# A three-layer decoder on one NeuronCore: one program block without barriers, and the FFN weights dequantised beside other work

## The chip, the cores and the metric

The kernel runs on one core of one Trainium2 chip. The metric is the device time of one execution in microseconds (us); lower is better. The profile is that of one execution on the same core. Engines in the profile: PE is TensorE (matmuls), PEld its weight loads, DVE is VectorE, ACT is ScalarE, POOL is GpSimd, SP is SyncE, which issues the transfers here.

## The reference

Inputs are `x` of 4 batches x 512 tokens x 512 features, fp32. Each of three layers ends in a residual sum and a LayerNorm.

```python
# 1: lightning attention: 16 heads of 32, chunks of 128 tokens, a decaying state kv carried over a batch's 4 chunks
q, k, v = rotary(x @ Wq), rotary(x @ Wk), x @ Wv
inter = (q * q_decay) @ kv;  intra = ((q @ k.T) * dmask) @ v
kv = r_C * kv + (k * k_decay).T @ v
x = layernorm(x + rms_norm(attn, rms_w) @ Wo)
# 2: one expert a batch: two int8 "smooth quant" linears, weights fside (512x512) and ctx (512x256)
h = smooth_quant_linear(x, fside);  gate, up = split(h)
x = layernorm(x + smooth_quant_linear(silu(gate) * up, ctx))
#    smooth_quant_linear: s = sqrt(colmax|x| / colmax|w|); x/s and w*s are scaled by row, rounded, clipped, multiplied, rescaled
# 3: FFN with fp4 weights: packed nibbles -> table value * fp16 scale of each group of 128 inputs; I = 1408
h = silu(x @ Wg.T) * (x @ Wu.T);  y = h @ Wd.T;  y = y / rms(y)
x = layernorm(x + y)
```

## The kernel before

Tokens lie on partitions in chunks of 128; a batch has four chunks (NC), the whole input sixteen. A product that must keep fp32 precision is three passes over operands split into a rounded part (`_hi`) and a remainder (`_lo`): ACT copies the rounded part out of PSUM, DVE subtracts it from the same PSUM bank to give the remainder. PSUM has eight banks of 128x512 fp32, `ps[0]` to `ps[7]`. Each engine has its own instruction stream, written out by hand, and executes it in order; what must follow what on another engine is a semaphore wait. Three program blocks follow each other, with a barrier of all engines between them:

- `attention_phase` (L574) runs the 16 chunks of layer 1. Beside them it places the steps of layer 2 for batch 0, by the table `EXPERT0_STEPS` (chunk, part 0 to 2). It also decodes the fp4 nibbles to fp8 values, a sixteenth of them in each chunk (`decode`, `scale_values`), into `shared`. The last chunk is n = 15. After it DVE and ACT finish the LayerNorm of batch 3 of layer 1 (x1), in `z`, and SP stores it.
- `weight_phase` (L1187) makes the FFN weights in 35 pieces: POOL (for some pieces ACT) builds diagonal matrices of the group scales, `scale_diag`; PE multiplies four fp8 blocks with four diagonals into a bank (L1257), which transposes and scales them; ACT writes the hi part (L1240) and DVE the lo part (L1248). Bank m % 8 serves piece m.
- `ffn_phase` (L1263) goes through four batches of 11 inner tiles `it`. For each, PE makes `gate` (12 matmuls, bank 4), `up` (12 matmuls, bank 5) and the `down` product of the tile before (12 matmuls, banks 0 to 3); ACT applies silu, DVE multiplies by up, ACT and DVE split the result into h_hi and h_lo. PE has three places a tile for other work, one after each of these groups of 12, so 33 places a batch, numbered `at` = 3*it + 0, 1, 2. There the steps of layer 2 for the next batch are placed, by the table `EXPERT_STEPS` (name: place), and the output steps of the batch before. On ACT and DVE the same places stand between the silu, multiply and split steps. At the end of a batch PE transposes the next batch's input (`transpose_x2`, L1522). Batches 1 and 2 are a hardware loop.

The steps of layer 2 use two PSUM banks, 6 and 7, in turn, in the order of the list `EXPERT_USES`. Each use waits until the one before it on that bank is drained (`start_use`, `drained`), which is done by the engine that reads the bank: DVE for `ratio` and `scale_x`, ACT for the transposed integers, and so on.

Names that come up again: `rows` broadcasts the column factors into both banks for `scale_x` and `scale_w` (DVE); `max_x`, `max_w` are row maxima (DVE); `round_x`, `round_w` are four activations each (ACT); `clip_x`, `clip_w` are POOL's; `xq01` to `wq23` transpose the integers and ACT copies them out; `w_scale`, `v_scale` broadcast a weight's row scales into a bank. The second linear has the same steps with `a` and `v`.

Of the kernel before, what the change touches and what calls it, by code (L numbers as in the profile page):

```python
# [15 lines left out]
F8 = mybir.dt.float8e4  # L16

# [113 lines left out]
LINKS = 14  # L131


QUAD = 4


def weight_pieces():


    pieces = []  # L140
    for t in range(0, GU_TILES, QUAD):
        for g in range(NK):
            pieces.append(("gu", g, t * P, min(QUAD, GU_TILES - t), t * E + g * P, E, g * GU_TILES + t))
    for k in range(NI):
        pieces.append(("dn", k, 0, NK, GU_TILES * E + k * P, I, NK * GU_TILES + k * NK))
    return pieces


PIECES = weight_pieces()


class Expert:

    def __init__(self, nc, sem, memory):
# [15 lines left out]
        self.gated, self.summed = sem("gated"), sem("summed")  # L170
        self.x2_shift, self.x2_done, self.mom = sem("x2_shift"), sem("x2_done"), sem("e_moments")
# [1447 lines left out]
```

## Time and profile before

| | |
|---|---|
| median of 3 runs (lowest to highest) | 849.53 us (847.71 to 850.36) |
| the profiled execution: device time, span | 849.56 us, 847.8 us |
| busy share of the span | PE 87%, PEld 70%, DVE 54%, ACT 43%, POOL 25% |
| mean granted TensorE clock | 0.942 |
| instructions | 11955 |

The span runs from the first to the last instruction. A timeline row gives the start in us, the length in us, engine, line, operation, what it writes and reads, how many instructions were merged (x4), and in square brackets the idle time of that engine just before it and who ended it. In a row of windows the five "busy (count)" pairs are PE, PEld, DVE, ACT and POOL; behind them stand the granted clock of TensorE (1.00 is 2.4 GHz, 0.50 is 1.2 GHz), the share of DMA busy and GB/s. "L12" is a line of the kernel before. Matmuls overlap, so that the length of one (0.39 us for 128x512) is more than the distance between two.

### The profile page before, as it was taken

To read this page: it belongs to the slowest core of one execution; us is meant where nothing else is said; L and a number is where in the kernel's file an instruction comes from. 1 tells how busy PE (TensorE), PEld (TensorE's weight loads), DVE (VectorE), ACT (ScalarE), POOL (GpSimd) and SP (SyncE) were. 2 spreads that over 40 slices of the span, in tenths; PEclk is the share of its full clock that TensorE was granted. 3 is DMA by queue.
4 is the path that set the end of the run, shared out by engine and by line. 5 is a ranking of instruction groups with operands and counts; after the bars stand their busy time and mean duration, and the time that the engine had idled before them with its cause. 6 is when DMAs were issued, how large, how long until landed. Compare 5 with 4: busy or idle time off the path is not lost.

```text
span 847.8 us, 11955 instructions
## 1 busy us (share of the span) xinstructions
PE 738.6 (87%) x4662; PEld 597.1 (70%) x4662; DVE 459.4 (54%) x899; ACT 362.3 (43%) x583; POOL 212.1 (25%) x242
## 2 busy tenths in 40 slices
PE   5899989989997994269999989999979998899993
PEld 4688867778875783137877767877767777688882
DVE  4567567765656757376725346745358444433214
ACT  4353343555444362573532453543463625431312
POOL 1453444445334353390101210110200111200000
PEclk9899999999999998558999989999999999999997
DMA  8400100023011100401020120030120020100201
GB/s 310 174 27 1 39 13 14 2 84 104 2 26 63 50 2 1 148 1 51 1 74 1 50 99 1 1 124 0 49 99 0 24 99 1 50 1 1 100 0 49
DMA packets 25402, 41.08 MB, mean 48 GB/s; under 512 B 5002, under 2 KB 7690, under 8 KB 25226
## 3 DMA queue, kind: packets, MB, share of 16 engines
q1 hardware_dynamic: 23194, 37.40, 13.2%
q10 hardware_dynamic: 2160, 3.02, 1.0%
q8 instruction: 33, 0.54, 0.3%
q14 instruction: 15, 0.12, 0.0%
HBM read 28.88 MB, written 11.53 MB: 48 GB/s over the span
## 4 chain that ended last, share of the span: by engine, by line
PE 42%; DVE 6%; ACT 4%; issue 2%; DVEq 0%; ACTq 0%
PE ps L1498 27%; PE ps L1508 10%; PE ps L477 2%; DVE silu L1431 1%; PE ps L468 1%; DVE act_s L318 1%; PE ps L457 1%; ACT silu L1356 1%; ACT h_hi L1339 1%; ACT xb L248 1%; DVE xc L1444 1%; ACT q2T L224 0%; DVE e_stats L399 0%; PE ps L1522 0%; PE ps L449 0%
## 5 line engine op out<-in xcount | busy, mean ns | idle before, releaser
L1498 PE MATMUL ps<-x2T_lo,wgu_hi 128*128 128x512 f32 x352 | 143.6, 408 | 5.2 <-DVE x2T_lo L1421 5.2
L1498 PE MATMUL ps<-x2T_hi,wgu_lo 128*128 128x512 f32 x352 | 139.1, 395 | 0.0
L1498 PE MATMUL ps<-x2T_hi,wgu_hi 128*128 128x512 f32 x352 | 139.1, 395 | 0.0
L1431 DVE TENSOR_TENSOR silu<-ps,silu 128x512 f32<-128x512 f32 x44 | 30.4, 691 | 136.0 <-PE ps L1498 130.8
L1080 PE MATMUL ps<-wqkv_lo,xT_hi 128*128 128x512 f32 x192 | 81.8, 426 | 9.3 <-DVE wqkv_lo L960 5.7
L1498 PEld LDWEIGHTS ps<-x2T_lo,wgu_hi 128*128 128x128 f32 x352 | 67.7, 192 | 20.9 <-DVE x2T_lo L1421 6.2
L1498 PEld LDWEIGHTS ps<-x2T_hi,wgu_lo 128*128 128x128 f32 x352 | 67.2, 191 | 14.6
L1498 PEld LDWEIGHTS ps<-x2T_hi,wgu_hi 128*128 128x128 f32 x352 | 67.5, 192 | 13.6
L1080 PE MATMUL ps<-wqkv_hi,xT_hi 128*128 128x512 f32 x192 | 76.8, 400 | 0.0
L1080 PE MATMUL ps<-wqkv_hi,xT_lo 128*128 128x512 f32 x192 | 76.7, 399 | 0.0
L1345 ACT ACTIVATE silu<-ps 128x512 f32<-128x512 f32 x44 | 26.2, 595 | 114.7 <-PE ps L1498 114.7
L897 POOL TENSOR_TENSOR rot<-qkv,tab 128x256 f32<-128x256 f32 x64 | 44.6, 730 | 117.9 <-ACT qkv L810 117.9
L1339 ACT ACTIVATE h_hi<-silu 128x512 fp32r<-128x512 f32 x44 | 27.8, 631 | 105.9 <-DVE silu L1431 105.8
L1508 PE MATMUL ps<-wdn_lo,h_hi 128*128 128x512 f32 x176 | 70.0, 398 | 0.0
L1508 PE MATMUL ps<-wdn_hi,h_lo 128*128 128x512 f32 x176 | 68.7, 390 | 0.0
L1508 PE MATMUL ps<-wdn_hi,h_hi 128*128 128x512 f32 x176 | 68.5, 389 | 0.0
L280 POOL TENSOR_SCALAR act_s<-act_s 128x1024 f32<-128x1024 f32 (+1 forms) x16 | 13.3, 830 | 183.6 <-ACT act_s L218 183.4
L1011 DVE TENSOR_TENSOR masked<-ps,mask 128x512 f32<-128x512 f32 x64 | 39.8, 684 | 32.0 <-PE ps L1118 32.0
L1080 PEld LDWEIGHTS ps<-wqkv_lo,xT_hi 128*128 128x128 f32 x192 | 37.3, 194 | 20.0 <-DVE wqkv_lo L960 6.1
L810 ACT ACTIVATE qkv<-ps 128x512 f32<-128x512 f32 x48 | 28.6, 597 | 51.3 <-PE ps L1080 51.3
L1415 DVE TENSOR_TENSOR h_lo<-silu,h_hi 128x512 fp32r<-128x512 f32 x44 | 30.5, 694 | 32.9 <-ACT h_hi L1339 32.9
L1257 PE MATMUL ps<-scale_diag,shared 128*128 128x128 f16 x132 | 19.3, 308 | 27.6 <-POOL scale_diag L1220 27.6
(168 smaller groups left out, 1519.3 us busy)
## 6 DMA issues: line engine op xcount, KB each, us to landing
w<-in_fside_BxS2xS_dram SPq DMA_DIRECT2D x4, 1024.0 KB, 6.4
x_dram<-xb SPq DMA_DIRECT2D x4, 1024.0 KB, 4.5
xc<-x_dram SPq DMA_DIRECT2D x4, 1024.0 KB, 5.9
x_in<-in_x_dram SPq DMA_DIRECT2D x15, 256.0 KB, 3.1
xb<-x_dram SPq DMA_DIRECT2D x3, 1024.0 KB, 5.5
out_dram<-xc SPq DMA_DIRECT2D x3, 1024.0 KB, 4.3
z<-in_x_dram SPq DMA_DIRECT2D x3, 768.0 KB, 5.0
x_dram<-z SPq DMA_DIRECT2D x3, 768.0 KB, 4.0
```

The costliest lines, as they stand in the source:

```text
L477: last = nc.tensor.matmul(self.bank(use)[:, :], q1T[:, k, c * P:(c + 1) * P], q2T[:, k, :], start=(k == 0), stop=(k == kt - 1))
L810: nc.scalar.activation(qkv[:, n % 2, p * E:(p + 1) * E], bank(u, n)[:, :], ACT.Copy)\
L897: nc.gpsimd.tensor_tensor(rot[:, m], v, f, ALU.mult).then_inc(rot_a, 1)
L1011: nc.vector.tensor_tensor(masked[:, j], in_groups(f"s{j}", n), mask[:, j], ALU.mult)\
L1080: last = nc.tensor.matmul(bank(u, n)[:, :], lhs, rhs, start=(k == 0 and m == 0), stop=(k == NK - 1 and m == 2))
L1257: last = nc.tensor.matmul(ps[m % len(ps)][:, t * P:(t + 1) * P], values[:, start + t * stride:start + t * stride + P], scale_diag[:, m % D ...
L1339: nc.scalar.activation(h_hi[:, it % 2, :], silu[:, it % 2, :], ACT.Copy).then_inc(h_hi_done, 1)
L1345: nc.scalar.activation(silu[:, it % 2, :], ps[4][:, :], ACT.Silu).then_inc(silu_done, 1)
L1415: nc.vector.tensor_tensor(h_lo[:, it % 2, :], silu[:, it % 2, :], h_hi[:, it % 2, :].bitcast(F32), ALU.subtract).then_inc(h_lo_done, 1)
L1431: nc.vector.tensor_tensor(silu[:, it % 2, :], ps[5][:, :], silu[:, it % 2, :], ALU.mult)\
L1498: last = nc.tensor.matmul(dst[:, :], lhs, rhs, start=(k == 0 and n == 0), stop=(k == NK - 1 and n == 2))
L1508: last = nc.tensor.matmul(ps[c][:, :], lhs, rhs, start=(it == 0 and n == 0), stop=(it == NI - 1 and n == 2))
```

## The change

The three blocks become one, without a barrier. Each engine runs its attention program and then its FFN program. Four things move:

1. Memory is laid out by hand: `weights`, the hi and lo parts of all FFN weights, lies over the buffers of attention (`wqkv`, `xT`, `mask`, `kv`, `wo`, `z` and others), so a piece may be written only when what lies below it is done. Piece 24 on lies over `z` and waits for the store of x1.
2. The weight phase is gone. Its 35 pieces are placed among other work: 0 to 5 in the last chunk (`PIECES_BESIDE`, banks 2 to 4), 6 to 34 at places 0 to 28 of the first FFN batch (`PIECE_STEPS`), on the banks 6 and 7 of layer 2. POOL makes all diagonals, into four buffers instead of eight: 0 to 3 after chunk 14, 4 to 6 after chunk 15, and then piece m+1's at the place of piece m, behind the clip and gate steps of that place.
3. The last part of x1's LayerNorm for batch 3 runs at place 1 of the first FFN batch on ACT and DVE (`late`); SP's stores of it now stand ahead of its first FFN transfers. The second batch's fside weight is loaded in the last chunk.
4. The steps of layer 2 are retimed: `w_scale` and `v_scale` come before the integers, the second linear's steps up to one place earlier, the sums `xb + act_s` of batches 1 to 3 go from POOL to DVE, `normalise` from place 31 to 30. The hardware loop is written out. In chunk 15 the residual of the chunk stands ahead of the expert's sums on DVE, and the rms root ahead of its normalise on ACT.

```diff
-                "round_w": 10, "clip_w": 10, "xq01": 13, "xq23": 14, "wq01": 15, "wq23": 16, "w_scale": 16,
+                "round_w": 10, "clip_w": 10, "w_scale": 11, "xq01": 13, "xq23": 14, "wq01": 15, "wq23": 16,
...
-                "clip_v": 25, "aq": 27, "vq": 28, "v_scale": 28, "y01": 29, "rescale_y01": 29, "add01": 29, "y23": 30,
-                "rescale_y23": 30, "add23": 30, "sum01": 30, "sum23": 31, "e_root": 31, "shift": 31, "normalise": 31}
+                "clip_v": 25, "v_scale": 25, "aq": 26, "vq": 27, "y01": 28, "rescale_y01": 28, "y23": 29,
+                "rescale_y23": 29, "sum01": 29, "sum23": 29, "e_root": 30, "shift": 30, "normalise": 30}
...
+PIECES_BESIDE = {(15, 0): (0, 1), (15, 1): (2, 3), (15, 2): (4, 5)}
+PIECE_BANKS = (3, 4, 3, 4, 3, 2)
+FIRST_BESIDE = len(PIECE_BANKS)
+PIECE_STEPS = {m - FIRST_BESIDE: m for m in range(FIRST_BESIDE, len(PIECES))}
+LATE_PIECE = 24
+ROWS_OPEN = range(13, 21)
+DIAGS = 4
...
+def expert_bank(use):
+    if use[0] == "piece":
+        return (use[1] + (use[1] in ROWS_OPEN)) % 2
+    return EXPERT_USES.index(use[1]) % 2
...
+    def diagonals(self, pool, m):
+        if m >= DIAGS:
+            _, full, _, at = self.use(m - DIAGS)
+            pool.wait_ge(full, at + 1)
...
+    def product(self, pe, m):
+        kind, where, k, tiles, _ = PIECES[m]
+        bank, full, drained, at = self.use(m)
+        pe.wait_ge(self.diag_done, m + 1)
+        if at > 0:
+            pe.wait_ge(drained, at)
+        for n in range(self.count(m)):
...
+            last = self.nc.tensor.matmul(bank[:, n * P:(n + 1) * P], values, self.diag[:, m % DIAGS, n, :],
+                                         start=True, stop=True)
+        last.then_inc(full, 1)
+    def hi(self, act, m):
+        act.wait_ge(full, at + 1)
+        if m == LATE_PIECE:
+            self.wait_last_x1(act)
+        self.nc.scalar.activation(self.parts(m)[0], bank[:, 0:self.count(m) * P], ACT.Copy).then_inc(self.hi_done, 1)
+    def lo(self, dve, m):
+        dve.wait_ge(self.hi_done, m + 1)
+        self.nc.vector.tensor_tensor(lo, bank[:, 0:self.count(m) * P], hi.bitcast(F32), ALU.subtract)\
+            .then_inc(drained, 1)
...
         def sums(b, chunks):
             for c in chunks:
+                if b > 0:
+                    self.wait_drained(dve, b, f"y{c}")
+                    nc.vector.tensor_tensor(xb[:, c, :], xb[:, c, :], act_s[:, c, :], ALU.add).then_inc(self.summed, 1)
...
+            if n == CHUNKS - 2:
+                for m in range(DIAGS):
+                    weights.diagonals(pool, m)
+        for m in range(DIAGS, FIRST_BESIDE + 1):
+            weights.diagonals(pool, m)
...
+    def place(expert_steps, output_steps, b, piece=None, late=()):
+        def run(at):
...
+            if b == 0 and piece and at in PIECE_STEPS:
+                piece(PIECE_STEPS[at])
+            if b == 0 and at == 1:
+                for step in late:
+                    step()
...
+        for b in range(B):
+            transpose_x2(b)
+            beside = place(steps, {}, b, lambda m: weights.product(pe, m))
+            for it in range(NI):
+                inner_tile(b, it, beside)
+            down(b, NI - 1)
```

Three places show the new order. The rows are instructions of one engine, with the semaphores that each waits for.

POOL at the end of the last chunk, before (`sq` is the squares' sum, `xb` the sum of layer 2):

```order
L927 TENSOR_TENSOR sq<-sq 128x256 [waits ps1_drained]
L929 TENSOR_TENSOR sq<-sq 128x128 [waits sq_halved]
L291 TENSOR_TENSOR xb<-xb,act_s 128x512 [waits bank6_drained]
L291 TENSOR_TENSOR xb<-xb,act_s 128x512 [waits bank7_drained]
L580 UNCONDITIONAL_BRANCH
```

POOL there now:

```order
L1080 TENSOR_TENSOR sq_65<-sq_65 128x256 [waits ps1_drained]
L1082 TENSOR_TENSOR sq_65<-sq_65 128x128 [waits sq_halved]
L340 TENSOR_TENSOR xb<-xb,act_s 128x512 [waits bank6_drained]
L340 TENSOR_TENSOR xb<-xb,act_s 128x512 [waits bank7_drained]
L690 TENSOR_TENSOR scale_diag_95<-ident_ones,scale_cols_78 128x512 [waits ps3_full]
L690 TENSOR_TENSOR scale_diag_95<-ident_ones,scale_cols_78 128x512 [waits ps4_full]
```

The two new rows are the diagonals of pieces 4 and 5. PE's products of these pieces stand ahead of the last chunk's output product `y` (L1324).

PE at place 7 of the first FFN batch, before (`rows`, then `down`):

```order
L457 MATMUL ps6<-ident_ones,small 128x128 [waits columns_ready,bank6_drained]
L457 MATMUL ps6<-ident_ones,small 128x128 x3
L457 MATMUL ps7<-ident_ones,small 128x128 [waits columns_ready,bank7_drained]
L457 MATMUL ps7<-ident_ones,small 128x128 x3
L1508 MATMUL ps0<-wdn_lo,h_hi 128x512 [waits h_lo_done]
```

PE there now:

```order
L505 MATMUL ps6<-ident_ones,small 128x128 [waits columns_ready,bank6_drained]
L505 MATMUL ps6<-ident_ones,small 128x128 x3
L505 MATMUL ps7<-ident_ones,small 128x128 [waits columns_ready,bank7_drained]
L505 MATMUL ps7<-ident_ones,small 128x128 x3
L707 MATMUL ps6<-scale_diag_95,values_gu_76 128x128 [waits bank6_drained,w_diag_done]
L707 MATMUL ps6<-scale_diag_95,values_gu_76 128x128 x3
```

Piece 13's product comes directly behind the rows, on the same bank 6.

SP's first transfers after the last chunk's, before and now:

```order
L1317 DMA xb<-x1_dram 128x4x512 [waits x2T_ps,x2_stored]
L1320 DMA w<-in_ctx_1024_dram 128x4x256 [waits bank7_full]
```

```order
L921 DMA x2_dram<-xb 128x4x512 [waits x2_done]
L878 DMA x1_dram<-z_75 128x512 [waits x1_done]
L878 DMA x1_dram<-z_75 128x3x512 [waits x1_done]
L1395 DMA xb<-x1_dram 128x4x512 [waits x2T_ps,x2_stored]
L1398 DMA w<-in_ctx_1024_dram 128x4x256 [waits bank6_full]
```

The load of the next batch's x1 now stands behind the two stores of batch 3's x1, which wait for the LayerNorm that was moved to place 1.

## Rows read from the trace of the kernel before

**Rows 1.** Windows of core 0: length, engines' busy time (count), PEclk, DMA share, GB/s.
```profile
352.20:383.20 31.00, 19.29 (x132) 11.60 (x133) 21.74 (x35) 23.46 (x53) 28.68 (x30) 0.50 0.21 68
386.50:502.30 115.80, 107.78 (x519) 86.69 (x517) 57.50 (x97) 48.29 (x79) 14.12 (x13) 0.99 0.13 41
502.30:515.20 12.90, 12.90 (x49) 10.46 (x50) 8.04 (x12) 6.63 (x9) 0.00 (x0) 0.85 0.26 83
623.70:634.80 11.10, 11.10 (x49) 9.16 (x50) 8.13 (x12) 6.66 (x9) 0.00 (x0) 1.00 0.29 94
```

**Rows 2.** Timeline of PE after the last chunk: start, length, engine, line.
```profile
353.25 1.61 PE L1257 MATMUL ps<-scale_diag,shared 128*128 128x128 f16 x12 [18.57 <-POOL scale_diag L1220]
383.22 3.65 PE L1522 MATMUL ps<-ident_ones,xb 128*128 128x128 f32 x16 [1.68 <-PEq L1196]
```

**Rows 3.** Timeline of ACT, last chunk.
```profile
331.52 0.60 ACT L854 ACTIVATE sq<-ps 128x512 f32<-128x512 f32 x1 [0.76 <-DVE o_lo L1023]
333.78 2.05 ACT L818 ACTIVATE shared<-magnitude 128x1056 fp8e4<-128x1056 f16 x1 [1.67 <-DVE magnitude L953]
338.84 2.93 ACT L248 ACTIVATE xb<-xb,small 128x512 f32<-128x512 f32 x4 [0.44 <-DVE small L408]
```

**Rows 4.** Timeline of POOL, last chunk.
```profile
332.19 0.99 POOL L927 TENSOR_TENSOR sq<-sq 128x256 f32<-128x256 f32 x1 [4.06 <-ACT sq L854]
334.03 2.50 POOL L291 TENSOR_TENSOR xb<-xb,act_s 128x512 f32<-128x512 f32 x2
```

**Rows 5.** Timeline of DVE, last chunk.
```profile
333.67 1.27 DVE L399 BATCH_NORM_STATS2 e_stats<-xb 128x6 f32<-128x512 f32 x2
341.95 0.16 DVE L970 RECIPROCAL rms<-rms 128x1 f32<-128x1 f32 x1 [3.14 <-ACT rms L862]
```

**Rows 6.** Lines of the weight phase: count, duration ns min/median/max, starts, shapes.
```profile
L1220 POOL TENSOR_TENSOR scale_diag<-ident_ones,shared x30: 620/1048/1052, 352.2 to 379.8; 128x512 f16<-128x512 f32 x27, 128x256 f16<-128x256 f32 x3
L1257 PEld LDWEIGHTS ps<-scale_diag,shared x132: 102/149/152, 353.2 to 381.1; 128*128 128x128 fp8e4 x132
L1240 ACT ACTIVATE wgu_hi<-ps x24: 378/594/598, 353.9 to 371.4; 128x512 fp32r<-128x512 f32 x20, 128x256 fp32r<-128x256 f32 x4
L1248 DVE TENSOR_TENSOR wgu_lo<-ps,wgu_hi x24: 415/687/693, 354.5 to 372.1; 128x512 fp32r<-128x512 f32 x20, 128x256 fp32r<-128x256 f32 x4
```

**Rows 7.** DMA issues of the page: count, KB each, us to landing.
```profile
xb<-x_dram SPq DMA_DIRECT2D x3, 1024.0 KB, 5.5
```

**Rows 8.** Timeline of DVE, batch 0, from its maxima of x1.
```profile
396.39 2.00 DVE L318 TENSOR_REDUCE act_s<-xb 128x256 f32<-128x1024 f32 x1
408.99 2.48 DVE L350 TENSOR_TENSOR act_s<-xb,ps 128x512 f32<-128x512 f32 x4
414.12 2.45 DVE L350 TENSOR_TENSOR w<-w,ps 128x512 f32<-128x512 f32 x4
```

**Rows 9.** Timeline of PE, batch 0: rows, wq23, columns2.
```profile
406.72 1.03 PE L457 MATMUL ps<-ident_ones,small 128*128 128x128 f32 x8
434.82 1.03 PE L468 MATMUL ps<-ident_ones,w 128*128 128x128 f32 x8
457.45 0.38 PE L449 MATMUL ps<-ident_ones,act_s 128*128 128x128 f32 x2
```

**Rows 10.** Timeline of ACT, batch 0.
```profile
414.23 2.94 ACT L218 ACTIVATE act_s<-act_s,biases,small 128x512 f32<-128x512 f32 x4 [0.38 <-DVE small L366]
436.35 1.25 ACT L224 ACTIVATE q2T<-ps,biases 128x512 bf16<-128x512 f32 x2
472.17 2.08 ACT L218 ACTIVATE w<-w,biases,small 128x256 f32<-128x256 f32 x4 [2.31 <-DVE small L366]
```

**Rows 11.** Timeline of DVE, batch 0, second layer.
```profile
459.81 0.75 DVE L323 TENSOR_REDUCE small<-ps 128x2 f32<-128x256 f32 x2
```

**Rows 12.** Waits of the whole run: us in total, times, longest.
```profile
PE ps L457 <- ACT q2T L224: 8.8, 7, 1.4
```

**Rows 13.** Timeline of PE, end of batch 0.
```profile
498.14 2.49 PE L1522 MATMUL ps<-ident_ones,xb 128*128 128x128 f32 x16 [2.59 <-ACT xb L248]
```

More of the change, by code:

```diff
@@ new lines @@
+USES_OF = {"columns": ("x_colmax", "w_colmax"), "rows": ("x_rows", "w_rows"), "w_scale": ("w_scale",),
+           "xq01": ("xq0", "xq1"), "xq23": ("xq2", "xq3"), "wq01": ("wq0", "wq1"), "wq23": ("wq2", "wq3"),
+           "products01": ("gate_up0", "gate_up1"), "products23": ("gate_up2", "gate_up3"),
+           "columns2": ("a_colmax", "v_colmax"), "rows2": ("a_rows", "v_rows"), "v_scale": ("v_scale",),
+           "aq": ("aq0", "aq1"), "vq": ("vq0", "vq1"), "y01": ("y0", "y1"), "y23": ("y2", "y3")}
@@ L538, in attention_order, with pieces @@
 def attention_order():
+    def pieces(n, part):
+        return (("piece", m - len(PIECES)) for m in PIECES_BESIDE.get((n, part), ()))
     yield from (("xT", 0), ("q", 0), ("k", 0), ("xT", 1), ("v", 0), ("q", 1), ("k", 1))
@@ new lines, in attention_programs, with const @@
+    ident_ones, raw, xb, ps = (memory[name] for name in ("ident_ones", "raw", "xb", "ps"))
+    (x_in, z, tab, mask, rms_col, wqkv_hi, wqkv_lo, wo_hi, wo_lo, halves, magnitude, sign, xT_hi, xT_lo, qkv, kd, rot,
+     kT_hi, kT_lo, qT_hi, qT_lo, qdT, masked, kv_old, kv, o_hi, o_lo, sq, rms, stats, mv, ln) = (
+        memory[name] for name in ATTENTION_TILES)
+    eps = expert.biases[:, 0:1]
+    def const(name):
+        return tab[:, TABLE[name][0] - 2 * P:TABLE[name][1] - 2 * P]
+    ident, ones = ident_ones[:, 0, :], ident_ones[:, 1, :]
@@ new lines, in wait_full, with wait_drained, drain_sem, state_ready @@
+    def wait_full(eng, u, n):
+        m, at = ATTENTION_USE[u, n]
+        eng.wait_ge(full[m], at + 1)
+    def wait_drained(eng, u, n):
+        m, at = ATTENTION_USE[u, n]
+        eng.wait_ge(drained[m], at + 1)
+    def drain_sem(u, n):
+        return drained[ATTENTION_USE[u, n][0]]
+    def state_ready(eng, n):
+        b, c = divmod(n, NC)
+        if c == 0:
+            wait_drained(eng, "kv", n)
+        else:
+            eng.wait_ge(kv_done, b * (NC - 2) + c)
+    def beside(steps, n, part):
+        for name, place in EXPERT0_STEPS.items():
+            if place == (n, part) and name in steps:
+                steps[name](0)
@@ new lines, in beside_pieces, with load_half @@
+    def beside_pieces(step, eng, n, part):
+        for m in PIECES_BESIDE.get((n, part), ()):
+            step(eng, m)
+    def load_half(eng, n, weight, half):
+        ks = slice(half * KH, (half + 1) * KH)
+        eng.dma_start(raw[:, n, ks], weight.rearrange("(k p) n -> p k n", p=P)[:, ks]).then_inc(wqkv_in[n][half], 16)
+    gu_words = a["L0_ffn_gate_up_packed"].rearrange("(t p) w -> p t w", p=P).bitcast(U16)
+    dn_words = a["L0_ffn_down_packed"].rearrange("(t p) w -> p t w", p=P).bitcast(U16)
```

1813 lines of the change are left out of this document (901 added, 912 removed).

## The prediction, made before the changed kernel was run

> **What bounds the kernel now.** I read the windows by stage first, then the timelines around the seams, then those of the first FFN batch. In the FFN TensorE is the bound: in the 115.8 us of the first batch it is busy 107.8 us at a granted clock of 0.99, while DVE, ACT and POOL work 57.5, 48.3 and 14.1 us [rows 1]. There, what PE gets in addition costs its full time, and what the others get costs only where PE waits for them. The weight phase is the opposite: 31.0 us at clock 0.50 (1.2 GHz), with POOL busy 28.7 us of it [rows 1]. Ahead of it PE had been idle 18.57 us [rows 2], through the end of layer 1 on ACT and DVE and a barrier. PE's FFN work starts with the transposes at 383.22 [rows 2]. So the seam is worth much. The question is what the 35 pieces cost in the places they get.
>
> **The seam: what goes.** Times are those of the trace before. In the last chunk pieces 0 to 3 come ahead of the attention product: four products and a wait for bank 4, about 1.9 us later than before (my estimate: 4 x 0.3, and 0.7 for the bank). The square on ACT, before at 331.52 [rows 3], then ends at about 334.0. POOL follows with its two squares' sums (332.19 to 334.03, 1.8 us) and the expert's sums, 2.50 us [rows 4], and only then come the diagonals of pieces 4 and 5, 1.05 us each [rows 6]: 340.6. PE stands in front of these pieces with its output product behind them. After the products, ACT's and DVE's parts take until 342.6; the decode on DVE takes 2.3 us (the square starts at 331.52 and the conversion, which waits for the decode, at 333.78) and the conversion 2.05 us [rows 3]: 347.0. Then the rms root (0.3), residual and its statistics (1.7), the expert's four statistics (2 x 1.27 [rows 5]), 1.7 us of small steps, and normalise, 2.93 us [rows 3]: 356.2. Without the order on POOL it would be some 6 us earlier, but DVE's residual, before at 341.95 and behind the expert's sums [rows 5], now also stands ahead of them. Gain: 383.22 - 356.2 = 27.0 us. The transposes after it start at the low clock as before, since PE idles there again.
> The moved `v_scale` and `w_scale` save 0.9 us more in attention: PE waited for ACT ahead of L457 7 times for 8.8 us in all [rows 12], one of them there.
>
> **The products.** A piece is four matmuls of 128 columns. At clock 0.50 one takes 0.149 us of weight load [rows 6]; at full clock I take half, 0.3 us a piece. Bounds: 0.2 us, a quarter of what 512 columns take (11.1 us for 49 of them is 0.227 each [rows 1]), and 0.6 us, the low clock. 27 pieces' worth in the first batch (29, of which four are half) are 8.1 us (5.4 to 16).
>
> **What the first batch waits for.** On ACT a piece costs 0.59 us, on DVE 0.69, on POOL 1.05 [rows 6]: 17, 20 and 30 us more, which the idle time of the three would hold. What it doesn't hold is the order: a product stands in PE's stream with its wait, and PE goes no further until the bank is free and the diagonal built. A group of 12 matmuls is 2.72 us (12 x 0.227). I walk the queues with the durations of the rows, t = 0 at the first gate matmul.
> - Places 1 to 6. Maxima of w (2.0 us, as those of x1 [rows 8]) stand ahead of a piece on DVE, and the late LayerNorm on ACT (2.9 us, as normalise [rows 3]): PE waits 1.5 and 1.6 us at places 3 and 4. The late LayerNorm ends at 14.1; SP stores it and only then issues the load of x1, which takes 5.5 us [rows 7] and lands at 20.0. Before, DVE began the maxima of x1 at 396.39 [rows 8], t = 10. Now it stands at them until 20.1, with piece 9's lo part behind, whose bank the product at place 5 needs: 4.5 us. The second maxima follow: 1.7 us at place 6 and 0.4 for piece 12. Sum 9.7.
> - Places 7 and 8. The rows end at 406.72 + 0.8 [rows 9], and `scale_x`, which drains their bank, ran from 408.99 for 2.48 us, to 411.5 [rows 8]. Piece 13 is on that bank: 4.0 us and some issue. Piece 14 waits for `scale_w`, before at 414.12 for 2.45 us [rows 8], with the row maxima ahead of it. PE's next group is only 2.7 us: another 4.0. Sum 8.1.
> - Places 10 and 11. The diagonals of pieces 16 and 17 stand on POOL behind `clip_x` and `clip_w`, and these behind four activations, 2.94 us [rows 10]: 2.9 and 2.2 us. Sum 5.1.
> - Places 13 to 18. Six pieces behind transposes or products on the same bank. An example is wq23: PE at 434.82 [rows 9], drained by ACT at 436.35 + 1.25 [rows 10], so 2.0 us after the transposes' end. In all 2.0, 0.4, 0.7, 2.1, 0.2, 1.1: sum 6.5.
> - Places 22 to 24. Column maxima's transposes at 457.45 [rows 9], their bank drained at 459.81 + 0.75 [rows 11]: 2.6 us; then `scale_a` 1.6 and `scale_v` 0.8. Sum 5.0.
> - Places 25 to 28. `v_scale` is drained by ACT behind `round_v`, 2.08 us [rows 10], and that behind h_hi: 4.0 us. Then 0.3, 1.3, 2.2. Sum 7.8.
>
> The stalls are 42.2 us. They take the place of three waits that the batch had, 3.8 us by the same timelines. The batch's end: normalise now stands on ACT ahead of the last tile's h_hi, and the shift on DVE ahead of its multiply, behind sums which DVE now adds itself (4 x 0.6). So h_lo comes 12.6 us after the last gate began, where PE is ready after 8.2: a stall of 4.4 us. In return the transposes no longer wait for normalise (2.59 us before [rows 13]) and the splits come earlier: together -0.4 us. First batch: 8.1 + 42.2 - 3.8 - 0.4 = +46.1 us.
>
> **The other batches.** In the second and third, `w_scale` and `v_scale` no longer wait 1.3 us each ([rows 12], 8.8 / 7); at `v_scale` about 1 us comes back, since max_w's twin and round_v stand ahead. With the 0.4 at the end, 2.1 us each: -4.2. The last batch is unchanged.
>
> **The sum** against the profiled execution, 849.56 us (the median of the runs is 849.53): 849.6 - 27.0 - 0.9 + 46.1 - 4.2 = 863.6. I forecast 864 us.
>
> **A rule on the clock.** The same 49 matmuls took 11.1 us at clock 1.00 and 12.9 us at 0.85, where PE had waited for the transposes' splits before [rows 1]: 1.8 us for one fall. The sum has none of that in it.
> The Trainium skill ("TensorE: Matmul & The Clock Gate", "A second HAM failure mode: psum-queue depth-cycling") says that PE's small idle times between groups, while it cycles through PSUM banks, can make its clock swing between the two levels. That is the order this change makes, and the 12.9 us row agrees with the direction. By the rule the sum would be that of the third rival below, by the row of the first batch (0.99 in spite of small waits) that of the forecast.
>
> **Rivals.**
> 1. The pieces hide. If the products find banks and diagonals ready, the first batch pays only 8.1 us and still loses its 3.8 us of waits: 849.6 - 27.9 + 8.1 - 3.8 - 0.4 - 4.2 = 821 us. For it: the idle time of ACT, DVE and POOL. Against it: the pairs of rows above show the drains after PE's arrival. The place that decides is the first batch, and the change is faster than before when its stalls stay under 42.2 - 14.0 = 28 us.
> 2. Half of the stalls. They are chained, and a wait at one place may pay for the next: 21 us gives 842 us.
> 3. The clock falls at each stall of 4 us or several small ones. Ten falls of 1.8 us: 882 us. For it the 0.85 row; against it that DVE, not PE, sets the time in those stretches.
> 4. The barrier wasn't the cost: the seam keeps more than I think, if PE stands longer behind pieces 4 and 5. The 18.57 us of idle ahead of the weight phase [rows 2] would stay, and only 31.0 - 12 = 19 us go: 872 us. It lies within the range of the forecast.
>
> **Numbers.** Forecast with rival 4: 0.60, own range 852 to 876. Rival 3: 0.14. Rival 2: 0.14, of which 0.02 within 0.3%, since it lies near the border. Rival 1: 0.08. The remaining 0.04 is a coincidence of gains and stalls, no change. A measurement of this kernel tells apart about 0.3%, 2.5 us. Faster: 0.12 + 0.08 = 0.20; same: 0.02 + 0.04 = 0.06; slower: 0.74. The range, 842 to 882, leaves out rival 1 and half of each of its neighbours, about 2 in 10.
>
> **What would show it.** The transposes of the first batch start near 355 (right) or well before 350 (the diagonals of 4 and 5 didn't hold PE). PE's waits list products behind DVE's scaling steps (4 us each at places 7 and 8) and behind POOL. The load of x1 is issued 14 us after the batch's start, and the maxima of x1 start at t = 20. The first batch lasts 160 us instead of 115.8, and the next ones about 2 us less than before. The forecast is wrong if the first batch stays under 144 us.

## The result, and the profile after

| | before | changed |
|---|---|---|
| median (lowest to highest), same chip | 849.37 us (847.71 to 850.36) | 875.33 us (873.02 to 875.97) |
| profiled execution: device time, span | 849.56, 847.8 us | 875.86, 873.2 us |
| mean granted clock | 0.942 | 0.942 |
| first gate matmul of batch 0, 1, 2, 3 (us) | 386.5, 502.3, 623.7, 741.4 | 358.7, 532.5, 650.7, 767.9 |

The changed kernel is slower: ratio 1.0303, 95% interval 1.0284 to 1.0321. The sign and the range of the forecast were right; the rise is 26 us where 14.5 were forecast. By the last line of the table the FFN begins 27.8 us earlier (forecast 27.9), the first batch takes 173.8 us instead of 115.8 (+58.1; forecast +46.1), the next two 3.8 us less together (forecast 4.2), and the last one 1.1 less (forecast 0). So one stage holds the error. The mean granted clock is the same by coincidence: the 31 us at 0.50 of the weight phase are gone, and the first batch has fallen from 0.99 to 0.90.

The batches as windows of the changed kernel (length; busy time and count of PE, PEld, DVE, ACT, POOL; clock; DMA share; GB/s), to be laid beside [rows 1]:

```profile
358.70:532.50 173.80, 132.29 (x625) 101.48 (x624) 79.81 (x132) 66.04 (x112) 33.34 (x34) 0.90 0.10 35
532.50:650.70 118.20, 110.03 (x515) 87.63 (x517) 68.30 (x121) 54.07 (x85) 9.02 (x9) 0.97 0.14 49
```

PE's idle time in the first batch is 173.8 - 132.3 = 41.5 us, where it was 115.8 - 107.8 = 8.0. That is 33.5 of the 58.1 us. The other 24.5 us are busy time of PE, at a clock of 0.90 instead of 0.99. Of these the forecast had 8.1, for the products of the pieces. What the lower clock costs it had left out.

PE at the seam (start, length; in brackets the idle time ahead and who ended it), which answers to [rows 2]:

```profile
338.21 0.61 PE L707 MATMUL ps<-scale_diag,values_dn 128*128 128x128 f16 x4 [6.85 <-POOL scale_diag L690]
339.58 0.78 PE L1324 MATMUL ps<-wo_lo,o_hi 128*128 128x512 f32 x1
344.81 0.28 PE L1330 MATMUL ps<-ident_ones,sq 128*128 128x1 f32 x2
355.63 3.30 PE L1581 MATMUL ps<-ident_ones,xb 128*128 128x128 f32 x16 [10.54 <-ACT xb L297]
358.68 0.48 PE L1551 MATMUL ps<-x2T_lo,weights 128*128 128x512 f32 x1
```

The transposes start at 355.63 (forecast 355.3). PE stood 6.85 us for the diagonal of piece 4, as forecast. The twelve matmuls of the output product behind it took 5.2 us (339.58 to 344.81), at the low clock.

PE in the first batch, rows with long waits, and rows of the groups that follow (`values_dn`, `values_gu` with `scale_diag` is a piece's product):

```profile
370.16 0.38 PE L707 MATMUL ps<-scale_diag,values_gu 128*128 128x128 f16 x4 [2.18 <-DVE weights L724]
370.35 0.47 PE L1551 MATMUL ps<-x2T_lo,weights 128*128 128x512 f32 x1
374.61 0.38 PE L707 MATMUL ps<-scale_diag,values_dn 128*128 128x128 f16 x4 [1.25 <-DVE weights L724]
...
384.84 0.59 PE L707 MATMUL ps<-scale_diag,values_dn 128*128 128x128 f16 x4 [7.00 <-DVE weights L724]
385.18 0.78 PE L1551 MATMUL ps<-x2T_lo,weights 128*128 128x512 f32 x1
389.86 1.04 PE L497 MATMUL ps<-ident_ones,act_s 128*128 128x128 f32 x8
...
399.26 0.52 PE L707 MATMUL ps<-scale_diag,values_gu 128*128 128x128 f16 x4 [3.85 <-DVE act_s L397]
399.54 1.20 PE L1565 MATMUL ps<-weights,h_hi 128*128 128x512 f32 x2
406.26 0.59 PE L707 MATMUL ps<-scale_diag,values_gu 128*128 128x128 f16 x4 [2.21 <-DVE w L397]
406.60 0.78 PE L1551 MATMUL ps<-x2T_lo,weights 128*128 128x512 f32 x1
410.85 0.40 PE L707 MATMUL ps<-scale_diag,values_gu 128*128 128x128 f16 x4
...
446.59 0.38 PE L707 MATMUL ps<-scale_diag,values_dn 128*128 128x128 f16 x4 [1.89 <-ACT q2T L273]
446.78 0.88 PE L1565 MATMUL ps<-weights,h_hi 128*128 128x512 f32 x2
451.43 1.67 PE L525 MATMUL ps<-q2T,q1T 128*128 128x512 bf16 x7
...
474.44 0.37 PE L707 MATMUL ps<-scale_diag,values_gu 128*128 128x128 f16 x2 [2.56 <-DVE small L370]
480.91 0.27 PE L707 MATMUL ps<-scale_diag,values_gu 128*128 128x128 f16 x2 [1.38 <-DVE act_s L397]
491.36 0.27 PE L707 MATMUL ps<-scale_diag,values_gu 128*128 128x128 f16 x2 [3.62 <-ACT scale_row L278]
...
525.99 1.22 PE L1565 MATMUL ps<-weights,h_hi 128*128 128x512 f32 x2 [3.49 <-DVE h_lo L1478]
530.28 1.91 PE L1581 MATMUL ps<-ident_ones,xb 128*128 128x128 f32 x16
```

Two things are to be read here. The waits are where the prediction put them. And most long waits have a slow group of 12 matmuls behind them: 385.18 to 389.86, 406.60 to 410.85, 525.99 to 530.28. At full clock a group lasts 2.72 us. Nine waits of the first batch are of 2 us or more. Behind eight of them the group took 4.1 to 4.7 us. Behind the one at place 3 (2.18 us) it took 3.0 (370.35 to 374.61 less the next wait of 1.25). A ninth slow group, of about 4.5 us, is the one at place 16, behind a wait of 1.89 us, while the group behind the 1.89 us at place 13 took 2.8. So the length of one wait does not tell by itself whether the clock falls.

SP and DVE around the load of x1, which answers to [rows 7] and the first of [rows 8]:

```profile
373.77 0.42 SPq L1395 DMA_DIRECT2D xb<-x_dram  x1
```

```profile
382.21 1.89 DVE L365 TENSOR_REDUCE act_s<-xb 128x256 f32<-128x1024 f32 x1 [7.74 <-DMA xb<-x_dram]
```

The load is issued 15.1 us after the batch's start (forecast 14), but 8.4 us pass from issue to DVE's first maximum, where I took 5.5. So DVE begins at t = 23.5, not at 20.

### The profile page after: what moved, and what is told of

It reads as the page before. It is cut to its first block, busy times and chain, and to the rows that moved or that the text cites. A ratio compares the mean times of both kernels' runs of the same rounds, so it can differ in the third digit from the quotient of the medians.

```text
span 873.2 us, 11695 instructions
## 1 busy us (share of the span) xinstructions
PE 744.7 (85%) x4652; PEld 600.2 (69%) x4662; DVE 469.2 (54%) x911; ACT 357.1 (41%) x566; POOL 201.4 (23%) x235
## 4 chain that ended last, share of the span: by engine, by line
PE 60%; DVE 21%; ACT 10%; DMA 4%; issue 3%; POOL 1%; ACTq 0%; SPq 0%; DVEq 0%
PE ps L1551 21%; PE ps L1565 11%; PE ps L1240 11%; PE ps L1324 3%; PE ps L1279 3%; PE ps L525 2%; DMA rms_col<-in_L_attn_rms_w_dram 2%; DVE small L404 2%; PE ps L516 2%; DVE masked L1169 2%; DVE act_s L365 2%; PE ps L1307 1%; DVE act_s L397 1%; ACT h_hi L1418 1%; PE ps L1264 1%
## 5 line engine op out<-in xcount | busy, mean ns | idle before, releaser
L1551 PE MATMUL ps<-x2T_hi,weights 128*128 128x512 f32 x704 | 219.7, 393 | 0.0
L1551 PEld LDWEIGHTS ps<-x2T_hi,weights 128*128 128x128 f32 x704 | 133.9, 190 | 27.4
L1551 PE MATMUL ps<-x2T_lo,weights 128*128 128x512 f32 x352 | 143.4, 407 | 0.9 <-DVE x2T_lo L1484 0.9
L1565 PE MATMUL ps<-weights,h_hi 128*128 128x512 f32 x352 | 122.0, 430 | 10.4 <-DVE h_lo L1478 10.4
L1494 DVE TENSOR_TENSOR silu<-ps,silu 128x512 f32<-128x512 f32 x44 | 30.3, 689 | 118.2 <-PE ps L1551 118.1
L1565 PEld LDWEIGHTS ps<-weights,h_hi 128*128 128x128 f32 x352 | 71.7, 210 | 26.5 <-DVE h_lo L1478 11.7
L1551 PEld LDWEIGHTS ps<-x2T_lo,weights 128*128 128x128 f32 x352 | 67.1, 191 | 15.1 <-DVE x2T_lo L1484 1.6
L1565 PE MATMUL ps<-weights,h_lo 128*128 128x512 f32 x176 | 73.7, 419 | 0.0
L724 DVE TENSOR_TENSOR weights<-ps,weights 128x512 fp32r<-128x512 f32 (+1 forms) x35 | 22.7, 657 | 55.4 <-ACT weights L717 55.3
L690 POOL TENSOR_TENSOR scale_diag<-ident_ones,scale_cols 128x512 f16<-128x512 f32 (+1 forms) x35 | 34.5, 1008 | 49.5 <-PE ps L707 49.0
L1240 PEld LDWEIGHTS ps<-wqkv_hi,xT_lo 128*128 128x128 f32 x192 | 36.7, 191 | 8.4
```

The costliest lines, as they stand in the source:

```text
L690: self.nc.gpsimd.tensor_tensor(diag, ident, cols.unsqueeze(len(shape) - 1).broadcast_to(shape), ALU.mult)\
L1240: last = nc.tensor.matmul(bank(u, n)[:, :], lhs, rhs, start=(k == 0 and m == 0), stop=(k == NK - 1 and m == 2))
L1494: nc.vector.tensor_tensor(silu[:, it % 2, :], ps[5][:, :], silu[:, it % 2, :], ALU.mult)\
L1551: last = nc.tensor.matmul(dst[:, :], lhs, rhs, start=(k == 0 and n == 0), stop=(k == NK - 1 and n == 2))
L1565: last = nc.tensor.matmul(ps[c][:, :], lhs, rhs, start=(it == 0 and n == 0), stop=(it == NI - 1 and n == 2))
```

## The experiments

In each the edit is to the changed kernel (875.33 us, first batch 173.8) unless it says otherwise. Ratios are to the kernel before on the same chip, with 95% intervals.

### e1_load_first: the load of x1 ahead of the late stores

```diff
-        for first in (True, False):
-            store_x1(B - 1, first)
+        return lambda: [store_x1(B - 1, first) for first in (True, False)]
...
                 sp.dma_start(xb[:, :, :], x1_v[b]).then_inc(expert.x1_in, 16)
+            if b == 1:
+                late_stores()
```

> SP issues the load of batch 1's x1 ahead of the two stores of batch 3's x1, nothing else changes. Theory of queued waits: DVE's 7.7 us of waiting for that load go, PE's 7.0 us wait ahead of piece 11 shrinks to at most 1 us, and the gate products behind it, which took 4.7 us, come back to 2.7 us: 7 to 10 us less than the changed kernel's 875.3, so 866 to 868 us. Rival (the waits are chained, what one gives up the next takes): the same time, within 2 us, with longer waits at places 7 and 8.

Measured: 866.87 us, ratio 1.0199 (1.0176 to 1.0222). The first batch takes 163.5 us, 10.3 less. On DVE the maxima of x1 now follow the work ahead of them without a wait:

```profile
376.13 1.97 DVE L365 TENSOR_REDUCE act_s<-xb 128x256 f32<-128x1024 f32 x1
```

The chain from the late LayerNorm over SP's stores to the load and on to PE's wait at place 5 is shown, with its price. The rival, that the next waits take what this one gives up, fell: places 7 and 8 wait 3.85 and 1.54 us here.

### e2_diagonals_early: diagonals 4 and 5 at the start of chunk 15

```diff
+            if n == CHUNKS - 1:
+                for m in range(DIAGS, FIRST_BESIDE):
+                    weights.diagonals(pool, m)
...
-        for m in range(DIAGS, FIRST_BESIDE + 1):
-            weights.diagonals(pool, m)
+        weights.diagonals(pool, FIRST_BESIDE)
```

> The diagonals of pieces 4 and 5 are built on POOL at the start of the last chunk instead of behind its sums. Theory of queued waits: PE's 6.85 us wait ahead of the last output product goes, the product runs at the full clock, and the first FFN batch starts 5 to 7 us earlier: 868 to 870 us. Rival (the end of the chunk hangs on POOL's and DVE's sums, not on PE): less than 2 us, since the expert's sums wait for POOL at 336.5 us anyway.

Measured: 872.91 us, ratio 1.0275 (1.0256 to 1.0294): only 2.4 us, between what the theory and its rival gave. PE no longer waits for piece 4, but the transposes start at 352.08, 3.6 us earlier and not 5 to 7. DVE during its last decode, and POOL beside it:

```profile
336.17 1.08 DVE L1106 TENSOR_SCALAR magnitude<-halves 128x264 uint16<-128x264 uint16 x1
337.17 1.08 DVE L1109 TENSOR_SCALAR sign<-halves 128x264 uint16<-128x264 uint16 x1
...
340.17 0.22 DVE L1106 TENSOR_SCALAR magnitude<-halves 128x264 uint16<-128x264 uint16 x1
```

```profile
332.41 0.74 POOL L1083 TENSOR_TENSOR sq<-sq 128x256 f32<-128x256 f32 x1 [4.41 <-ACT sq L1004]
333.65 2.51 POOL L340 TENSOR_TENSOR xb<-xb,act_s 128x512 f32<-128x512 f32 x2
336.11 4.06 POOL L690 TENSOR_TENSOR scale_diag<-ident_ones,scale_cols 128x512 f16<-128x512 f32 x4
```

The decode has eight such instructions, each 0.22 us in the kernel before. The four that run beside POOL's four diagonals take 1.08 us each, about the length of one diagonal, and the first one behind them takes 0.22 again. The two ahead of them, beside POOL's sums, took 0.97 and 1.30. That made a new theory, tested by e10.

### e10_hold_pool: e2, with POOL held until the decode has ended

```diff
+        pool.wait_ge(packed, CHUNKS)
         weights.diagonals(pool, FIRST_BESIDE)
```

> e2_diagonals_early with one wait more: POOL builds the diagonals from piece 6 on only after DVE's last decode has ended. In e2 the eight 16-bit TENSOR_SCALAR of the last decode ran beside POOL's sums and diagonals and took up to 1.08 us each, 7 us in all, where the same instruction takes 0.22 us beside an idle POOL. My theory (a busy POOL holds up this form of DVE's instructions): those that run after POOL's sums (2.5 us) take 0.22 us, the decode ends 3 to 4 us earlier, the transposes start at 348 to 349 instead of 352.1, and the kernel takes 872.9 - 3.5 = 869.5 us. Rival (the conversion waits for something else, or the diagonals of pieces 6 to 8 come late for places 0 and 1): no change, 873.

Measured: 868.50 us, ratio 1.0211 (1.0188 to 1.0233), an interval that lies wholly below that of e2. DVE:

```profile
335.44 1.30 DVE L1110 TENSOR_SCALAR sign<-halves 128x264 uint16<-128x264 uint16 x1
336.66 0.22 DVE L1107 TENSOR_SCALAR magnitude<-halves 128x264 uint16<-128x264 uint16 x1
```

Only the two that run beside POOL's sums (334.14, 2.51 us) are slow. The transposes start at 349.13, 2.95 us earlier than in e2. The theory holds. The Trainium skill ("SBUF — State Buffer", "Who interferes with whom") says that `tensor_scalar` in a two-port mode and a GpSimd instruction exclude each other for a whole instruction. The 1.08 us beside a diagonal of about 1.0 us agree with that. That these instructions run in such a mode is shown by no run.

### e3_normalise_behind: normalise back from place 30 to 31

```diff
-                "rescale_y23": 29, "sum01": 29, "sum23": 29, "e_root": 30, "shift": 30, "normalise": 30}
+                "rescale_y23": 29, "sum01": 29, "sum23": 29, "e_root": 30, "shift": 30, "normalise": 31}
```

> normalise moves from place 30 to 31, behind the last tile's h_hi on ACT. Theory of queued waits: h_lo comes 2.9 us earlier, PE's wait ahead of the last down product falls from 3.5 to about 1 us at each of three batch ends, and the down product may come back to the full clock: 2 to 4 us a batch end, 863 to 869 us. Rival: the transposes then wait for normalise instead, as in the kernel before, and nothing is gained, 875 us.

Measured: 865.70 us, ratio 1.0195 (1.0170 to 1.0221). The 3.49 us wait at 525.99, which came at the end of three batches, is 1.27 us here, and the group behind it is no longer slow (2.9 us). The second and third batches take 114.7 us each instead of 118.2 and 117.3. In the changed kernel ACT did the normalisation (2.93 us) ahead of the last tile's h_hi, and PE needs h_hi first.

### e5_keep_busy: PE multiplies on while it waits

The extra matmuls write a bank that is free then, and nothing reads them. Their number follows each wait's length in the trace; PE takes the products later than that only by what a matmul in flight lasts.

```diff
+        def keep_busy(b, at, count):
+            it, slot = divmod(at, 3)
+            if slot == 0:
+                pe.wait_ge(h_done, b * NI + it)
+            else:
+                pe.wait_ge(silu_done, b * NI + it + 1)
+            bank = ps[4 if slot else 5]
+            for _ in range(count):
+                nc.tensor.matmul(bank[:, :], x2T_hi[:, 0, 0:P], x2T_hi[:, 0, :], start=True, stop=True)
...
+        FILL, FILL_LAST = {3: 8, 5: 26, 7: 15, 8: 9, 10: 10, 13: 7, 16: 7, 22: 9, 23: 5, 25: 14, 28: 8}, 13
```

> Ahead of 11 products of the first batch on which PE waits, and ahead of the last down product of batches 0 to 2, PE runs extra matmuls (5 to 26 of 128x512, together a little less than the wait) into a bank that is free there; all else is unchanged. Theory of the clock: the groups of 12 behind the waits, which took 4.1 to 4.7 us instead of 2.7, run at the full clock; 10 to 15 us less in all, 860 to 865 us, though PE does more. Rival (these groups are slow because ACT and DVE reach the same PSUM or because their operands are late): no gain, 875 us or more.

Measured: 862.16 us, ratio 1.0143 (1.0126 to 1.0160): 13.2 us less with 157 matmuls more. Here is PE around place 5, to be laid beside the three rows from 384.84 on of the changed kernel:

```profile
385.80 0.38 PE L707 MATMUL ps<-scale_diag,values_dn 128*128 128x128 f16 x4 [0.15 <-DVE weights L724]
385.99 0.47 PE L1551 MATMUL ps<-x2T_lo,weights 128*128 128x512 f32 x1
390.46 1.16 PE L497 MATMUL ps<-ident_ones,act_s 128*128 128x128 f32 x8 [1.46 <-DVE weights L724]
```

The group behind the product lasts 390.46 - 1.46 - 385.99 = 3.0 us instead of 4.7. The waited-for work comes no earlier, but PE is not slow behind it. The same stretch as a window, in the changed kernel and here:

```profile
395.00:425.00 30.00, 20.45 (x86) 15.68 (x85) 15.61 (x23) 12.13 (x18) 9.26 (x10) 0.83 0.00 1
```

```profile
395.00:425.00 30.00, 25.82 (x135) 20.25 (x134) 15.96 (x23) 12.94 (x20) 10.34 (x11) 1.00 0.00 1
```

The first batch takes 163.5 us, 10.3 less; the other 3 us come from the second and third batch, whose only change is at their ends. The clock after a wait is a cost by itself, and it is the missing term. It is not always paid in full: the wait at place 8 was 2.21 us and not the 4.0 forecast, because the slow group ahead of it had used up some 1.7. Here, where that group is fast, PE's products at place 8 stand 3.8 us behind the group's end (402.92 to 406.74, filled for 2.2 us).

### e6_no_pieces: pieces 6 to 34 left out

This kernel leaves out the dequantisation of these pieces. Later tiles multiply by the weights of pieces 0 to 5, so the time alone counts.

```diff
-            if b == 0 and piece and at in PIECE_STEPS:
-                piece(PIECE_STEPS[at])
...
-        m = PIECE_OF["gate_up", it // 2, k]
+        m = PIECE_OF["gate_up", 0, k]
```

> The changed kernel without pieces 6 to 34 (it leaves out the dequantisation of 9/11 of the FFN weights; later tiles use the weights of pieces 0 to 5). Measures what the pieces and all that they start cost. My theory: nearly the whole rise of the first batch (58.1 us, 115.8 -> 173.8) is their stalls, their products and the clock after the stalls; the batch then lasts 115.8 - 4 + about 7 for the late load of x1, which stays and now makes the column maxima late: 119 us, and the kernel 873 - 55 = 818 us (815 to 822). Rival (the retimed layer-2 steps or the one block cost time by themselves): above 830 us.

Measured: 826.19 us, ratio 0.9749 (0.9723 to 0.9775), outside the 815 to 822 of my theory. The first batch takes 126.1 us. The late load costs more than I wrote:

```profile
382.82 1.97 PE L495 MATMUL ps<-ident_ones,act_s 128*128 128x128 f32 x8 [10.03 <-DVE act_s L363]
```

So of the 58.1 us, 47.7 are the pieces (173.8 - 126.1) and 10.3 the rest, a net number. In it are this wait for the load of x1, the wait that the new place of normalise makes at the batch's end (3.48 us here too), and against them what the retimed steps give (2.7 us in e9, with the load on time and normalise at 31). That e1 took out 10.3 us as well, with the pieces in place, is a coincidence in part. My sentence that nearly all of it was the pieces is false by that sixth.

### e7_places: the same pieces at other places

```diff
-PIECE_STEPS = {m - FIRST_BESIDE: m for m in range(FIRST_BESIDE, len(PIECES))}
+PIECE_STEPS = {0: [6, 7], 1: [8, 9], 2: [10, 11], 3: [12], 4: [13], 9: [14], 10: [15], 11: [16], 12: [17, 18], 14: [19], 15: [20], 17: [21], 18: [22], 19: [23, 24], 20: [25, 26], 21: [27, 28], 24: [29], 26: [30, 31], 27: [32], 30: [33], 31: [34]}
...
-        return (use[1] + (use[1] in ROWS_OPEN)) % 2
+        return PIECE_BANK[use[1]]
...
-        for m in range(DIAGS, FIRST_BESIDE + 1):
+        for m in range(DIAGS, FIRST_BESIDE + 3):
```

> The same 29 pieces in the first batch at other places and on the bank that is drained first: two at places 0, 1, 2, 12, 19, 20, 21; none at 5, 7, 8, 13, 16, 22, 23, 25, 28; diagonals built three pieces ahead. My theory (a product costs the wait for its bank or diagonal, plus the low clock of the group behind it): the stalls at places 7, 8, 10, 13, 16, 22, 23, 25, 28 were 23.0 us in the changed kernel and go, with six falls of the clock of 1.7 us; some 6 us come back at 1, 2 and 12: 873 - 27 = 846 us (840 to 855). Rival (the stalls are the queues' own length on ACT and DVE and only move): 865 us or more.

Measured: 852.26 us, ratio 1.0039 (1.0008 to 1.0069), within my range and far below that of the rival. The first batch takes 151.5 us, 22.3 less, so most of the waits were a matter of place. What stayed are two waits for a bank whose lo part was late on DVE, 4.39 us for the late load of x1 at 391.84, and a down group that waits for its own weights (the third row):

```profile
372.81 1.18 PE L709 MATMUL ps<-scale_diag,values_dn 128*128 128x128 f16 x8 [4.99 <-DVE weights L726]
410.59 0.59 PE L709 MATMUL ps<-scale_diag,values_gu 128*128 128x128 f16 x4 [4.12 <-DVE weights L726]
502.02 1.19 PE L1568 MATMUL ps<-weights,h_hi 128*128 128x512 f32 x2 [5.70 <-DVE weights L726]
```

### e8_all_edits: e7 with the edits of e1, e2 and e3

> The new places of e7_places with the load of x1 first, the diagonals of pieces 4 and 5 early and the normalisation one place later. If the gains add: 873 - 27 - 8.5 - 2.4 - 9.6 = 826 us (820 to 838). Rival (they overlap: DVE is full in the first five places, with 8 us of maxima, 7 of pieces and 5 of its own in 16 us): 840 us or more.

Measured: 837.94 us, ratio 0.9886 (0.9837 to 0.9934): faster than before, at the upper end of my range. The gains did not add in full: e7, e1, e2 and e3 took out 23.1, 8.5, 2.4 and 9.6 us one by one, 43.6 in all, and together 37.4. The first two waits of e7 are here with the same 4.99 and 4.12 us. And the transposes of the profiled execution start at 355.49, not at the 352.08 of e2. Most of that arose ahead of any edit: POOL reaches the last squares' sum at 335.83 where it was 332.41, and the granted clock was 0.96 from 0 to 40 us and from 80 to 120, where it was 1.00 in e2. Why it fell there is open.

### e9_before_retimed: the kernel before, with the moved steps alone

The weight phase and the barriers stay. The edit is item 4 of the change, without the parts in chunk 15 and the unrolled loop, and with `normalise` at 31.

> The kernel before, with its weight phase and barriers, and only the moved steps of the second layer (v_scale, w_scale, sums on DVE), the normalisation at place 31. No piece in a batch. In the changed kernel with the same steps the second and third batches took 114.7 us against 121.4 and 117.7 before. My theory: 850 - 3.5 - 6.7 - 3.0 - 1 - 1 = 835 us (832 to 840). Rival (the gain of those batches came from the one block and not from these steps): 845 to 850.

Measured: 837.73 us, ratio 0.9863 (0.9831 to 0.9895). The batches take 113.1, 114.9 and 116.5 us, where they took 115.8, 121.4 and 117.7. So the retimed steps are worth 11.5 us without any piece beside a batch. In the second and third batch they give 7.8 us. The changed kernel got 3.8 there and e3 9.8, so normalise one place too early had cost it 6 us.

### e11_all_placed: e8 with the places mended

```diff
-PIECE_STEPS = {0: [6, 7], 1: [8, 9], 2: [10, 11], 3: [12], 4: [13], 9: [14], 10: [15], 11: [16], 12: [17, 18], 14: [19],
+PIECE_STEPS = {0: [6, 7], 2: [8, 9], 3: [10, 11], 4: [12], 5: [13], 9: [14], 10: [15], 11: [16], 12: [17], 14: [18, 19],
...
+        pool.wait_ge(packed, CHUNKS)
```

> All edits together, with the places mended after e8_all_edits: nothing at place 1 (PE goes from there to place 2 with no group between), the pieces of the third pair at places 3, 4, 5, 9 and 10, one piece fewer at 12, the last two at place 30 and e_root and shift at 31, round_w at 11, and POOL held until the decode has ended. e8 took 837.9 with stalls of 4.99, 4.12, 2.34 and 0.82 us at place 2, place 10 and the last two down groups. My theory: those go with 3 falls of the clock, and 3 us at the seam: 837.9 - 12.3 - 5 - 3 = 818 us; some 3 us come back where two pieces now stand: 821 us (816 to 828). Rival (DVE is full in places 0 to 5 and keeps PE waiting whatever the places): 832 or more.

Measured: 837.52 us, ratio 0.9859 (0.9836 to 0.9881), no better than e8, far from the 821 of my theory and in the range of its rival. The seam gained (transposes at 350.06), but the wait in the second tile grew, and its chain is not the one that I had named. PE, then ACT:

```profile
369.20 1.19 PE L709 MATMUL ps<-scale_diag,values_dn 128*128 128x128 f16 x8 [6.04 <-DVE weights L726]
```

```profile
364.93 2.93 ACT L980 ACTIVATE z<-z,ln 128x512 f32<-128x512 f32 x4 [3.58 <-DVE ln L1152]
367.76 1.05 ACT L719 ACTIVATE weights<-ps 128x512 fp32r<-128x512 f32 x2
```

DVE waits for the hi parts, and these stand on ACT behind the late LayerNorm, which waits for DVE's `ln` behind the maxima. With e_root and shift at place 31, normalise is late as well: PE waits 1.05 to 1.24 us for it ahead of the transposes and 2.16 behind them, at three batches' ends.

### e12_late_norm_moved: the late LayerNorm at place 4, e_root and shift back at 30

Two smaller moves go with it: piece 16 to place 12, and at place 30 the last two pieces ahead of the other steps.

```diff
-            if b == 0 and at == 1:
+            if b == 0 and at == 4:
                 for step in late:
...
-                "rescale_y23": 29, "sum01": 29, "sum23": 29, "e_root": 31, "shift": 31, "normalise": 31}
+                "rescale_y23": 29, "sum01": 29, "sum23": 29, "e_root": 30, "shift": 30, "normalise": 31}
```

> e11_all_placed with four changes read from its trace: the late LayerNorm of layer 1 at place 4 instead of 1 (in e11 it stood on ACT for 2.9 us ahead of the hi parts of pieces 8 and 9, and PE waited 6.04 us for them), piece 16 at place 12 (2.02 us at place 11), e_root and shift back at place 30 (2.16 and 1.05 us at the end of each of three batches), and the last two pieces ahead of them. My theory: 837.5 - 6.0 - 2.0 - 1.4 in the first batch - 2 falls of the clock of 1.7 - 3 x 1.5 for the batches' ends = 820 us (816 to 826). Rival (the chain through DVE's maxima, silu's product and h_lo holds the first two tiles anyway): 830 us or more.

Measured: 823.91 us, ratio 0.9693 (0.9677 to 0.9710), the fastest of all and within my range. The rival of e11 and of this run, that DVE keeps PE waiting whatever the places, falls with it. Its first batch as a window, and the longest wait left in it:

```profile
354.40:489.00 134.60, 119.20 (x626) 91.38 (x624) 79.53 (x131) 65.25 (x112) 33.46 (x34) 0.99 0.13 44
```

```profile
379.32 1.11 PE L499 MATMUL ps<-ident_ones,act_s 128*128 128x128 f32 x4 [2.70 <-DVE weights L726]
```

Against e9, whose layer-2 steps are nearly the same, the pieces cost 134.6 - 113.1 = 21.5 us in the first batch, and the FFN begins 387.2 - 354.4 = 32.8 us earlier. That is 11.3 us for the idea of the change when its waits are few. The medians of the two kernels are 13.8 us apart and the two profiled spans 12.7; the rest lies in the later batches, 1.4 us, and in the spread of the runs.

## Why the prediction was right in sign and too low

**The seam: right, 27.8 us for 27.9, partly by errors that cancel.** The path was the forecast one: POOL's diagonals, two pieces, DVE's decode, ACT's conversion, root, residual, normalise. The diagonals of pieces 4 and 5 were ready at 339.2, 0.5 us ahead of my 340.6 less the 0.9 saved before. The decode took 3.7 us (341.1 to 344.8) where I had 2.3, since two of its instructions took 1.15 and 1.08 beside POOL and not 0.22. What follows the conversion took 8.8 us where I had 9.2. The low clock of the output product cost nothing: PE had ended it at 345.1, and the root waited for ACT's conversion, until 346.8. Rival 4 (the seam keeps more) fell.

**The first batch: +46.1 forecast, +58.1 measured.** By PE's own time:

| term | forecast | measured | from |
|---|---|---|---|
| products of the pieces | 8.1 | 11.4 | e12's first batch at clock 0.99: 119.2 - 107.8 busy |
| PE's idle time | 42.2 - 3.8 - 0.4 = 38.0 | 33.5 | 41.5 - 8.0 |
| lower clock behind waits | 0 | 13.1 | 132.3 - 119.2 busy |
| sum | 46.1 | 58.0 | |

The first and the last row take e12 as the same work at full clock, though its order differs; e5 gives 10.3 us for the last one by another way, net of the waits that slow groups use up. The 11.4 us are not explained in full. In the trace of the changed kernel a product takes 0.20 us at full clock (391.33 to 391.53) and the group behind it 2.84 instead of 2.72, which for 27 pieces is some 8.6. The products, 3.3 too low, and the idle time, 4.5 too high, nearly cancel. With a clock that had stayed up the forecast would have looked better than its terms were.

**The step that failed is the clock.** The sum had none of it, and the third rival had it at ten falls of 1.8 us with a chance of 0.14. I argued against it that DVE, not PE, sets the time in those stretches. That is true of the wait itself and false of what comes behind it: PE has its 12 matmuls to do before it meets the next wait, and they took 1.4 to 2 us more each time. Nine such groups are 13 us. The truth lay between the forecast and that rival. The row of [rows 1] at 0.85 had shown the price; the argument, not the row, was wrong. 875.3 lies at the very edge of the 852 to 876 that I had given to a forecast without any loss by the clock, so that it is inside owes to the width and not to the mechanism. The rule of the Trainium skill ("TensorE: Matmul & The Clock Gate", "A second HAM failure mode: psum-queue depth-cycling"), which I had weighed and left out of the sum, pointed the right way. e5, where PE stayed busy at clock 1.00, agrees with it in that the idle time brings the fall. No run here changes the cycling through banks alone.

**The waits one by one.** Most were right within 0.4 us, these six among them: forecast 4.0, 2.9, 2.0, 2.6, 4.0 and 2.2 at places 7, 10, 13, 22, 25 and 28, and measured 3.85, 2.71, 1.89, 2.56, 3.62 and 2.12. Walking the queues with durations of the old trace worked here. Place 5 was too low (7.00 for 4.5), since the load of x1 took 8.4 us from issue to use, and place 3 by less (2.18 for 1.5). Places 6, 8 and 11 were too high (0.44 for 2.1, 2.21 for 4.0, 0.78 for 2.2), since the longer waits and slow groups ahead had paid for them. At place 11 e5, without the slow group, has 1.66. The wait at the batches' end was 3.49 for 4.4.

**The other batches** gained 3.8 us for 4.2. But the term was small only because a new wait of 3.5 us stood in each, with a slow group behind it (5.3 us at 643.2, 4.4 at 761.3): I had its price right and did not see that one place later it would be free (e3).

**Rivals 1 and 2** (hidden, or half of the waits) fell for this order. e8 and e12 show that they were a question of the table of places, which I had treated as given.

## What to carry to other kernels

A product put beside other work costs its own time, the wait for its bank, and the slow clock of whatever stands behind that wait; the third was as large as the first. Place such work by when a bank is drained and not one to a slot, and follow the whole chain back: the longest waits here ended at a store ahead of a load on SP and at a late LayerNorm on ACT. Take a change apart before you judge it: here the retimed steps alone were 11.5 us faster, and the block without barriers, with its pieces at better places, some 13 more, while the two together as written were 26 us slower.

## What the runs showed of the hardware

- A 16-bit TENSOR_SCALAR of DVE on 128x264 took 0.22 us beside an idle POOL and 1.08 beside POOL's TENSOR_TENSOR of about 1.0 us (e2, e10). Four of them beside four diagonals made the seam 2.95 us longer. Two of them beside POOL's sums took 0.97 and 1.30.
- POOL's sums of squares are held up in return: 0.99 us for 128x256 in [rows 4] beside DVE's decode, 0.74 us in e2 and e10.
- The decode's 16-bit TENSOR_TENSOR of 128x1056 took 1.13 us in the kernel before, beside those sums on POOL, and 0.71 in e10, beside an idle POOL.
- PE stayed at clock 1.00 from 395 to 425 us through waits filled with matmuls whose results nothing reads, where the window of the changed kernel has 0.83. Over the kernel the filled waits were worth 13.2 us (e5).
- The load of x1, 1 MB, took 8.4 us from issue to landing in the first batch of the changed kernel, right behind two stores of x1, the first issued 2.6 us ahead of it. In e1, with the stores behind it, the same load took 5.5 us.
